# Attention with a Hadamard transform and ternary weights on one core: the weight path and the first four batches rearranged

## The reference, cut to what matters

```python
q    = x + braak_embed[stage][..., None]         # one number added to each row of x
attn = softmax(q @ f.T)                          # f is key and value
xh   = (attn @ f) @ H
scale = clip(max|xh| per row, 1e-5) / 7
xq   = clip(round(xh / scale), -8, 7) * scale
w_scale = clip(mean|W| per row, 1e-5)
wq   = where(W/w_scale > .5, 1, where(W/w_scale < -.5, -1, 0)) * w_scale
out  = x + xq @ wq.T
```

## Time and profile before

| | us |
|---|---|
| median of 3 runs | 102.9 (101.88 to 104.1) |
| profiled execution, its own time | 102.76 |
| its span, first to last instruction | 100.9 |
| PE busy | 90.6 (90% of the span) |
| DVE, ACT, POOL busy | 79.1, 71.3, 70.9 |

### The profile page before, as it was taken

One profiled execution on the slowest core, in us unless ns is written; L12 is line 12 of the kernel. 1 busy time (PEld: TensorE's weight loads), 2 busy tenths in 40 slices (PEclk: granted clock), 3 DMA queues, 4 the chain that ended last, 5 costly groups with the idle time before them and its releaser, 6 DMA issues.

```text
span 100.9 us, 2542 instructions
## 1 busy us (share of the span) xinstructions
PE 90.6 (90%) x734; PEld 83.9 (83%) x734; DVE 79.1 (78%) x197; ACT 71.3 (71%) x185; POOL 70.9 (70%) x107
## 2 busy tenths in 40 slices
PE   5999898948599989999999999999999999999640
PEld 2379887948499979999999999999999999989410
DVE  1338597998549796988989797979796979798881
ACT  3558768775748796959596959695969595776820
POOL 4152270999778596959697979897889886505870
PEclk9999999999999999999999999999999999999999
DMA  2919804202758947464738473938283222321125
GB/s 74 300 71 317 300 6 113 101 0 104 161 154 263 107 119 226 134 206 133 226 98 265 113 251 82 282 93 270 63 292 82 86 53 103 66 97 44 60 107 205
DMA packets 14591, 14.71 MB, mean 146 GB/s; under 512 B 7922, under 2 KB 8568, under 8 KB 14584
## 3 DMA queue, kind: packets, MB, share of 16 engines
q1 hardware_dynamic: 14272, 14.36, 48.5%
q10 hardware_dynamic: 312, 0.27, 0.8%
HBM read 8.72 MB, written 4.19 MB: 128 GB/s over the span
## 4 chain that ended last, share of the span: by engine, by line
PE 68%; DVE 10%; DMA 7%; POOL 6%; issue 3%; ACT 3%; DVEq 0%; POOLq 0%
PE xh_bank L492 19%; PE score_bank L492 14%; PE fh_bank L492 12%; DMA code_t<-code 7%; PE out_bank L546 6%; PE q_bank L481 5%; PE prob_bank L481 5%; PE out_bank L461 4%; POOL code L371 2%; ACT q_hi L677 2%; POOL f_lo L331 1%; DVE q_lo L886 1%; POOL w_over_above L396 1%; DVE xh_bank L1028 1%; ACT code L681 1%
## 5 line engine op out<-in xcount | busy, mean ns | idle before, releaser
L703 ACT ACTIVATE prob<-score_bank,neg_max 128x256 f32<-128x256 f32 x30 | 13.9, 470 | 13.7 <-DVE neg_max L910 13.7
L379 POOL TENSOR_TENSOR result<-scaled,x_all 128x512 f32<-128x512 f32 x12 | 15.4, 1286 | 10.5 <-DVE scaled L872 10.5
L331 POOL TENSOR_TENSOR f_lo<-ft,f_hi 128x512 fp32r<-128x512 f32 x13 | 17.0, 1310 | 0.0
L845 DVE TENSOR_REDUCE abs_max<-xh_bank 128x2 f32<-128x512 f32 x14 | 9.7, 691 | 8.7 <-PE xh_bank L492 8.7
L492 PE MATMUL fh_bank<-had,f_hi 128*128 128x256 f32 x64 | 14.0, 300 | 0.0
L371 POOL TENSOR_TENSOR code<-code,magic 128x512 bf16<-128x512 f32 x13 | 13.5, 1041 | 0.5 <-ACT code L681 0.3
L681 ACT ACTIVATE code<-xh_bank,inv_scale 128x256 f32<-128x256 f32 x30 | 13.0, 498 | 0.4 <-DVE inv_scale L869 0.3
L492 PE MATMUL score_bank<-f_hi,q_hi 128*128 128x256 f32 x60 | 13.2, 301 | 0.0
L492 PE MATMUL fh_bank<-had,f_lo 128*128 128x256 f32 x64 | 12.7, 280 | 0.0
L872 DVE SCALAR_TENSOR_TENSOR scaled<-out_bank,out_scale,w_scale_row 128x256 f32<-128x256 f32 x27 | 11.8, 476 | 1.0 <-PE out_bank L546 1.0
L492 PE MATMUL xh_bank<-fh_hi,prob_hi 128*128 128x256 f32 x60 | 12.1, 283 | 0.1
(11 more groups left out here) (142 smaller groups left out, 228.2 us busy)
## 6 DMA issues: line engine op xcount, KB each, us to landing
ft<-f_turned_dram SPq DMA_DIRECT2D x16, 256.0 KB, 2.7
x_all<-x_dram SPq DMA_DIRECT2D x16, 256.0 KB, 2.8
out_dram<-result SPq DMA_DIRECT2D x14, 256.0 KB, 2.0
w_t<-weight_turned_dram SPq DMA_DIRECT2D x1, 256.0 KB, 3.0
out_dram<-result SPq DMA_DIRECT2D x2, 128.0 KB, 1.8
out_dram<-last_result ACTq DMA_DIRECT2D x2, 128.0 KB, 1.8
code_t<-code SPq DMA_TRANSPOSE x13, 2.5
had_block<-hadamard_dram SPq DMA_DIRECT2D x1, 64.0 KB, 2.9
```

What stands on the lines that cost most here:

```text
L331: nc.gpsimd.tensor_tensor(f_lo[:, b.k], ft[:, b.k], f_hi[:, b.k].bitcast(F32), ALU.subtract).then_inc(f_lo_ready, 1)
L379: nc.gpsimd.tensor_tensor(result[:, b.k], as_rows(scaled[:, b.k]), x_all[:, b.at], ALU.add).then_inc(result_ready, 1)
L703: a = nc.scalar.activation(prob[:, t], score_bank[:, t], ACT.Exp, bias=neg_max[:, b.k, t:t + 1], accum_out=row_sum[:, b.k, t:t + 1])
L845: nc.vector.tensor_reduce(abs_max[:, :], xh_bank[:, :, :], AX.X, ALU.max, apply_absolute_value=True).then_inc(abs_max_ready, 1)
```

## The change

The host passes W as it is. It is loaded with its rows on the partitions, so the row sums are one reduction on DVE and the scales are numbers per partition; signs are formed in that layout (tern), and one DMA transposition on SP, put between step 2 and step 3 of SP's list, turns them into tern_t. The row of scales comes from two PE transposes of the scales spread over 128 columns (`weight_row`), copied by DVE in step 4. POOL's four weight instructions, PE's four sums and the matrix of ones go.

The first batches: two of three Hadamard copies move from POOL to ACT, which has them ahead of its q of batch 0. PE makes tile 0 of f @ H of batch 0 before it turns q, tile 1 after. The scores of batch 0 go to two banks, one for each tile, each with its own maximum on DVE; the scores of batch 0 and of batch 1 begin before the low part of q is there. f @ H of batch 1 goes to side_bank. PE turns the exponentials of batch 0 ahead of the scores of batch 1, and q of batch 2 behind them. ACT takes the exponentials of batch 0 ahead of the split of q of batch 1. The low part of f of batch 2 moves from DVE to POOL. x of batch 2 is loaded as soon as x of batch 0 has landed, W behind f of batch 2. One product on zeros goes from each of the two places, and ACT's queue loads the stage numbers first.

```diff
-WARM = 8
-WARM_BETWEEN = 2
+WARM = 7
+WARM_BETWEEN = 1
@@ sync
-            sp.wait_ge(first_q_ready, 1)
-            sp.wait_ge(q_ready, 1)
+            sp.wait_ge(x_loaded[0], 16)
             sp.dma_start(x_all[:, 2], x_dram[2]).then_inc(x_loaded[0], 16)
-            sp.dma_start(w_t[:, :, :], weight_turned).then_inc(weight_loaded, 16)
             sp.wait_ge(early_f_lo_ready, 1)
             sp.dma_start(as_row(ft[:, 0]), ft_dram[2]).then_inc(ft_loaded[0], 16)
+            sp.dma_start(w_raw[:, :, :], weight_dram).then_inc(weight_loaded, 16)
...
-            for i in range(B + LAG_STORE - 2):
+            for i in range(3):
+                step(peeled(i))
+            sp.wait_ge(tern_ready, 1)
+            sp.dma_start_transpose(tern_t[:, :, :].rearrange("p c (t s) -> p (c t) s", t=T),
+                                   tern[:, :, :, :].rearrange("p c t d -> p (c t d)")
+                                   ).then_inc(tern_t_ready, 16)
+            for i in range(3, B + LAG_STORE - 2):
                 step(peeled(i), dma_turns=i - LAG_QUANT < turned_by_dma)
@@ gpsimd
-            nc.gpsimd.tensor_copy(had[:, :, 0:P], ...
             nc.gpsimd.tensor_copy(had[:, 0, P:D], had_block[:, :])
-            nc.gpsimd.tensor_scalar(had[:, 1, P:D], ...
...
             add_bias(Batch(0, 1))
             add_bias(Batch(0, 2))
-            weight_parts()
+            split_f(Batch(0, 2))
             add_bias(Batch(0, 3))
             least_scales(Batch(0, 0))
-            weight_bounds()
             step(peeled(3))
@@ tensor
+            def weight_row():
+                pe.wait_ge(w_wide_ready, 1)
+                for t in range(T):
+                    mm = pe.transpose(out_bank[:, 0, t * P:(t + 1) * P], w_wide[:, t], ident[:, :])
+                mm.then_inc(w_row_in_bank, 1)
...
             keep_warm(WARM_BETWEEN)
+            pe.wait_ge(early_f_lo_ready, 1)
+            pe.wait_ge(had_ready, 2)
+            pe.wait_ge(had_others_ready, 1)
+            hadamard_tiles(fh_bank, b0, [0])
             pe.wait_ge(first_q_ready, 1)
...
-            times_hadamard(b0)
-            for t in range(T):
-                pe.wait_ge(first_q_lo_ready, t + 1)
-                mm = product(score_bank, score_parts(b0), [t])
-            mm.then_inc(score_in_bank, 1)
+            hadamard_tiles(fh_bank, b0, [1]).then_inc(fh_in_bank, 1)
+            pe.wait_ge(first_q_hi_ready, 1)
+            product(first_score_banks[0], score_parts(b0), [0],
+                    wait_for_last_part=lambda: pe.wait_ge(first_q_lo_ready, 1)
+                    ).then_inc(first_score_in_bank, 1)
+            pe.wait_ge(q_hi_ready, 1)
+            product(first_score_banks[1], score_parts(b0), [1],
+                    wait_for_last_part=lambda: pe.wait_ge(first_q_lo_ready, 2)
+                    ).then_inc(score_in_bank, 1)
             turn_q(b1)
             pe.wait_ge(early_f_lo_ready, 2)
-            times_hadamard(b1)
+            hadamard_tiles(second_fh_bank, b1, range(T)).then_inc(fh_in_bank, 1)
+            turn_prob(b0)
+            pe.wait_ge(q_hi_ready, 2)
+            product(score_bank, score_parts(b1),
+                    wait_for_last_part=lambda: pe.wait_ge(q_lo_ready, 1)).then_inc(score_in_bank, 1)
             turn_q(b2)
-            turn_prob(b0)
-            score(b1)
             mix(b0)
-            weight_sums()
-            pe.wait_ge(early_f_lo_ready, 3)
             step(peeled(3))
+            weight_row()
             for stage, lag in STAGES_IN_ORDER:
                 if stage == times_ternary:
-                    pe.wait_ge(tern_t_ready, 1)
+                    pe.wait_ge(tern_t_ready, 16)
+                    pe.wait_ge(row_ready, 1)
@@ scalar
+            act.wait_ge(had_loaded, 16)
+            nc.scalar.copy(had[:, :, 0:P], ...).then_inc(had_ready, 1)
+            nc.scalar.activation(had[:, 1, P:D], had_block[:, :], ACT.Copy, scale=-1.0
+                                 ).then_inc(had_ready, 1)
...
+            split_f(b1)
             add_bias(b1)
-            split_f(b1)
             split_fh(b0)
             add_bias(b2)
+            for t in range(T):
+                act.wait_ge((first_neg_max_ready, neg_max_ready)[t], 1)
+                a = nc.scalar.activation(prob[:, t], first_score_banks[t][:, t], ACT.Exp, ...)
+            a.then_inc(prob_ready, 1)
             split_q(b1)
-            exponentials(b0)
-            split_q(b2)
             split_prob(b0)
             split_f(b2)
+            split_fh(b1, second_fh_bank)
+            add_bias(b3)
+            split_q(b2)
             exponentials(b1)
-            split_fh(b1)
-            add_bias(b3)
             split_f(b3)
@@ vector
+            def weight_sums():
+                nc.vector.tensor_reduce(w_sum[:, :], w_raw[:, :, :], AX.X, ALU.add,
+                                        apply_absolute_value=True).then_inc(w_sums_ready, 1)
+            def weight_scales():
...
+                nc.vector.tensor_scalar(w_scale[:, :], w_sum[:, :], 1.0 / D, MIN_ABS, ...)
+                nc.vector.tensor_scalar(w_half[:, :], w_scale[:, :], 0.5, None, ALU.mult)
+                nc.vector.tensor_copy(w_wide[:, :, :], w_scale[:, :].unsqueeze(2).broadcast_to([P, T, P]))
             def weight_signs():
...
+                for t in range(T):
+                    v = nc.vector.tensor_scalar(w_neg[:, t], w_raw[:, t], -1.0, w_half[:, t:t + 1],
+                                                ALU.mult, ALU.is_gt)
+                for t in range(T):
+                    v = nc.vector.scalar_tensor_tensor(
+                        out=tern[:, :, t], in0=w_raw[:, t]..., scalar=w_half[:, t:t + 1],
+                        in1=w_neg[:, t]..., op0=ALU.is_gt, op1=ALU.subtract)
+                v.then_inc(tern_ready, 1)
...
             split_f(b1)
+            dve.wait_ge(first_score_in_bank, 1)
+            nc.vector.tensor_reduce(neg_max[:, 0, 0:1], first_score_banks[0][:, 0], AX.X, ALU.max, ...)
+            dve.wait_ge(score_in_bank, 1)
+            nc.vector.tensor_reduce(neg_max[:, 0, 1:2], first_score_banks[1][:, 1], AX.X, ALU.max, ...)
             split_fh(b0)
-            maximum(b0)
             split_q(b1)
-            weight_sizes()
-            split_q(b2)
             split_prob(b0)
             inverse_sums(b0)
             maximum(b1)
-            split_f(b2)
+            split_q(b2)
+            weight_sums()
             for stage, lag in STAGES_IN_ORDER:
-                if b := peeled(3)(lag):
+                if stage == split_fh:
+                    split_fh(b1, second_fh_bank)
+                elif b := peeled(3)(lag):
                     stage(b)
                 if stage == scales:
-                    weight_rows()
+                    weight_scales()
             weight_signs()
-            for i in range(4, 2 * LOOP_FROM):
+            for stage, lag in STAGES_IN_ORDER:
+                if b := peeled(4)(lag):
+                    stage(b)
+                if stage == scales:
+                    weight_row()
+            for i in range(5, 2 * LOOP_FROM):
                 step(peeled(i))
```

More of the change, by code:

```diff
@@ L39, with adaln_ffn_kernel @@
 LAG_STORE = 5
-def adaln_ffn_kernel(nc, x, f_turned, itok, embed, weight_turned, hadamard, out):
+def adaln_ffn_kernel(nc, x, f_turned, itok, embed, weight, hadamard, out):
     B, S, D = x.shape
     STAGES = embed.shape[0]
-    O = weight_turned.shape[2]
+    O = weight.shape[0]
     T = S // P
@@ L55, in adaln_ffn_kernel @@
     out_dram = out.rearrange("b (p t) d -> b p (t d)", t=T)
+    weight_dram = weight.rearrange("(t p) d -> p t d", p=P)
     block_dram = hadamard[0:P, 0:P]
@@ L71, in adaln_ffn_kernel @@
         warm = sb("warm", [P, W], BF16)
-        ones = sb("ones", [P, P], F32R)
         had_block = sb("had_block", [P, P], F32)
         had = sb("had", [P, C, D], F32R)
-        w_t = sb("w_t", [P, C, O], F32)
-        w_abs = sb("w_abs", [P, C, O], F32)
-        w_scale_row = sb("w_scale_row", [P, O], F32)
[L78 to L83, removed]
+        w_raw = sb("w_raw", [P, T, D], F32)
+        w_sum = sb("w_sum", [P, T], F32)
+        w_scale = sb("w_scale", [P, T], F32)
+        w_half = sb("w_half", [P, T], F32)
+        w_wide = sb("w_wide", [P, T, P], F32)
+        w_neg = sb("w_neg", [P, T, D], F32)
+        w_scale_row = sb("w_scale_row", [P, O], F32)
+        tern = sb("tern", [P, C, T, P], BF16)
         tern_t = sb("tern_t", [P, C, O], BF16)
@@ L511, in score @@
             def score(b):
-                wait(pe, f_lo_ready, b.at - 2)
+                wait(pe, f_lo_ready, b.at - 1)
                 wait(pe, q_lo_ready, b.at)
@@ L527, in times_hadamard, with hadamard_tiles @@
             def times_hadamard(b):
-                wait(pe, f_lo_ready, b.at - 2)
+                wait(pe, f_lo_ready, b.at - 1)
                 wait(pe, fh_lo_ready, b.at)
-                product(fh_bank, [(f_hi[:, b.k], had), (f_lo[:, b.k], had)]).then_inc(fh_in_bank, 1)
```

(24 more changed lines are left out.)

90 lines of the change are left out of this document (37 added, 53 removed).

## The result

The changed kernel takes 105.85 us (median of 4 runs, 104.05 to 106.42), the kernel before beside it 103.37 (4 runs, 101.88 to 104.1): the ratio is 1.023 with an interval of 1.0125 to 1.033. Forecast were 101.5 and a range of 100.1 to 103.3. The profiled execution took 104.05 against 102.76, its span 102.2 against 100.9.

A forecast was written before the change was run, and what follows sets the result against it. PE, busy all 50.00 us from 40 to 90, was taken as the bound. An earlier times_ternary(0), 1.10, plus 0.58 for the slow turn, less 0.35 unexplained, gave a gain of 1.3: 102.76 to 101.5 us, range 100.1 to 103.3.

The forecast's parts named there:

- tern, both tiles / ready: DVE forms the weights' signs: two instructions, 0.74 us, with nothing beside them on POOL, ready at 20.22.
- codes' turn issued / its landing: SP's turn of batch 0's codes, behind the weights' turn and two loads: issued at 22.54, landing 3.0 us later.
- PE's wait before times_ternary(0): PE idle ahead of batch 0's first output product, until the codes' turn lands: 3.4 us.
- times_ternary(0) starts: PE's first output product, batch 0: 25.66 in place of 26.76, 1.10 us earlier.
- times_ternary(0) to times_ternary(2): Two PE steps of 44 products at 0.116 us each: 5.10 a step, 10.2 for two, in place of 10.78.
- The stall before turn_q(4): PE's wait for POOL's q of batch 4 (22.46 to 23.02): gone, with that q there at about 17.
- the 0.35 that I had kept as unexplained: Delay of times_ternary(0) in the kernel before that the count didn't explain; 0.35 us taken off the gain.
- the slow turn of the earlier trace: Turn for batch 2 in the kernel before, 4.26 us from 33.16: taken as gone, worth 0.58 us.
- A: Faster: codes' turn lands in 2.5 us despite loads ahead, times_ternary(0) at 25.2, gain 2.1, time 100.7; chance 0.22.
- B: Slower: weights' and codes' turns go one after the other, 4.26 us each; PE at 28.9, time 104.9; chance 0.07.
- C: Start: fewer products on zeros delay PE's rise in pace, costing up to 2.8 us, half of it 1.4: 102.9; chance 0.10.
- D: DVE's write of tern waits up to 0.9 us for POOL's code instruction: 102.4; chance 0.06.

The follow-up runs named there:

- busy waiting: Changed kernel with twelve products on zeros on PE ahead of its wait for the turned weights and codes of batch 0: 102.67 us, ratio 0.978 to the kernel before.
- the layout alone: Changed kernel with the weight path of the kernel before (weights turned by the host, POOL's four instructions): 103.29 us, ratio 1.005 to the kernel before.
- the start products back: Changed kernel with 8 and 2 products on zeros at the start, as in the kernel before: 104.72 us, ratio 1.018 to the kernel before.
- the longer wait: Kernel before with two more turns into a spare tile on SP ahead of the turn of the codes of batch 0: 106.36 us, ratio 1.023.

## Why the prediction was wrong

Up to the wait its count was right to within some 0.35 us; predicted and measured in the changed profile:

| step | predicted | measured |
|---|---|---|
| bias products start | 4.29 | 4.29 |
| scores of batch 0 end | 8.33 | 8.27 |
| wait for the low part of f @ H of batch 1 | 0.6 | 0.62 |
| tern, both tiles / ready | 0.74 / 20.22 | 0.88 / 20.19 |
| codes' turn issued / its landing | 22.54 / 3.0 | 22.66 / 3.20 |
| PE's wait before times_ternary(0) | 3.4 | 3.65 |
| times_ternary(0) starts | 25.66 | 25.99 |
| times_ternary(0) to times_ternary(2) | 10.2 | 12.77 |

The stall before turn_q(4) went (turn_q(4) at 19.88, no idle time ahead), the codes were kept back by SP, and the wait ended with the codes, not the weights. The waits of SP's queue (who waited, for whom: us, times, longest) name the price of its order:

```profile
SPq L301 <- DVE tern L842: 7.1, 1, 7.1
```

The 0.33 by which times_ternary(0) came late is the codes' turn, issued 0.12 later and landing 0.20 slower than counted; that it is close to the 0.35 that I had kept as unexplained is chance. So, in part, is the 20.19 for tern: DVE's unbroken stretch began at 13.09 in place of 13.37 and lasted 7.10 in place of 6.85.

**The step that failed** is in the sum: "A step is 44 products on PE, and 431 took 50.00 us, 0.116 each: 5.10 a step, 10.2 for two." I took a pace from 40 to 90 us, with the clock at 1.00, and put it behind a wait of 3.4 that the same text had worked out. I counted the wait by its length only. The first of the two steps took 7.65 (25.99 to 33.64 in PE's timeline), the second 5.12:

```profile
25.99 1.01 PE L532 MATMUL out_bank<-tern_t,code_t 128*128 128x256 bf16 x4 [3.65 <-DMA code_t<-code]
...
33.64 0.61 PE L532 MATMUL out_bank<-tern_t,code_t 128*128 128x256 bf16 x4
...
38.76 0.61 PE L532 MATMUL out_bank<-tern_t,code_t 128*128 128x256 bf16 x4
```

7.65 - 5.12 = 2.53 for the clock. The balance: times_ternary(0) 0.77 earlier than before (26.76 to 25.99), the slow turn of the earlier trace rows gone as forecast (0.55: 5.67 between the second and third output product before, 5.12 now), 2.53 lost: 1.21, and times_ternary(2) does start 1.22 later (38.76 against 37.54). That is the 1.3 of the span. Without the 2.53 the profiled execution would have ended 1.2 ahead of before's, at about 101.5 (an estimate; the fastest execution with busy waiting took 101.47).

**The rivals.** A fell by the landing of 3.20. B named the side on which the result fell, but its mechanism wasn't there: the two turns landed in 2.5 and 3.2. C had the right resource at the wrong place: I asked about PE's pace only at the start, and not behind the wait of 3.4 that the forecast itself had worked out. D fell: POOL was idle from 17.77 to 20.87, and tern took 0.48 for its first tile and 0.88 for both, where the earlier trace rows has 1.59. No rival had the wait's own cost, so the chance of slower, 0.08, was too small, and the upper end, 103.3, left out a loss of 2.5 on top of the forecast.

The Trainium skill speaks of this (TensorE: Matmul & The Clock Gate, "HAM oscillation — how this bites in real kernels"): in the loop of a large matmul, a wait for a DMA that is long enough makes the engine throttle, and the next work starts cold. This case's trace agrees: 0.50 from 24.76 to 31.59, around the end of a wait of 3.65. Rule and wait should have stood together as a rival of the slower side.

## What to carry to other kernels

Whoever works out a new wait of PE owes the pace behind it a line of its own: first how long PE idles, then what the granted clock does to the work that follows; here the second cost 2.53 us, more than the 1.1 us by which times_ternary(0) was to come earlier. Where a queue works in order, put the transfer whose data is ready first ahead of the one that must wait: one instruction moved on SP turned 2% slower into 3 to 5% faster. And before a part of a change is called worthless, look whether its profile started as the other did: the layout alone seemed to bring nothing, but its PE was some 2 us late from the start.

## What the hardware showed beyond that

**How long the clock stays low.** After waits of 3.65 and 3.73 it stood at 0.50 for 6.83 us, after one of 3.75 for 3.41, half as long; waits of 1.98 and 1.10 in the layout alone, and of 1.69 and 1.15 in the kernel before, left it at 1.00. The length isn't fixed for a kernel either: four of the six executions with the start products back have a mean clock of 0.954 or 0.955, one has 0.973 and one 0.998, and of the four with the longer wait three have 0.980 to 0.982 and one 0.957. Only one execution of each has a profile, so where the clock was low in the others isn't shown; a fall behind PE's last product, as in the changed kernel's profile from about 99.9 us on, makes up some 0.01 of such a mean.

**The start.** PE doubles its pace by 4.3 us in the changed kernel's profile, and at about 8.9 in that of the kernel with busy waiting, whose list up to there is the same. Two products of f @ H in the one and in the other:

```profile
5.48 0.40 PE L475 MATMUL fh_bank<-had,f_lo 128*128 128x256 f32 x2
```

```profile
6.09 0.63 PE L475 MATMUL fh_bank<-had,f_lo 128*128 128x256 f32 x2
```

The granted clock reads 1.00 in both, so only the products' durations show it. Among the profiles the rise came at about 4 to 5.4 or at 8.9 to 10.5, with nothing between; what decides isn't known.

**One slow turn.** The 4.26 of the earlier trace rows coincided with a fetch of 16 KB of instructions on another queue, at 34.4 us; that the fetch caused it isn't shown. No such turn is in the changed kernel, whose longest is the 3.20 behind two loads of 256 KB.
